# Attention with two chunks of scores at a time, their values and sums shifted, and output tiles in two parts

## What is computed

```
xn  = layernorm(x)
q   = xn @ q_w.T + q_b                       # 16 heads of 64
xd  = depthwise_conv(xn, width 3, stride 2)  # 2048 -> 1024 rows
k,v = xd @ k_w.T + k_b, xd @ v_w.T + v_b
att = softmax(q k^T / 8)                     # per head, 2048 x 1024
x1  = att v @ out_w.T + out_b
e   = argmax(xn @ W_router)                  # one of 4 experts per token
y   = gelu(xn @ W1[e] + b1[e]) @ Wo + bo + xn
out = x + x1 + layernorm(y) * ln_gamma + ln_beta
```

## Time and profile before

| | us |
|---|---|
| median of 3 runs | 1966.93 |
| lowest and highest | 1964.63, 2223.03 |
| the profiled execution | 1971.07 |
| its span, first to last instruction, slowest core | 1969.5 |
| spans of the eight cores | 1947.0 to 1969.5 |

### The profile page before, as it was taken

How to read it: one execution, slowest core, us unless ns; L and a number is a source line. 1 busy time by engine, 2 the same in 40 slices (tenths; PEclk the granted TensorE clock), 3 DMA queues, 4 the chain that set the end, 5 groups by cost and what they waited for, 6 DMA issues and landing times.

```text
span 1969.5 us, 37041 instructions; the slowest of 8 cores (1947.0 to 1969.5 us)
## 1 busy us (share of the span) xinstructions
PE 1828.8 (93%) x12540; PEld 1004.3 (51%) x12540; DVE 934.0 (47%) x1257; ACT 895.2 (45%) x1381; POOL 298.3 (15%) x357
## 2 busy tenths in 40 slices
PE   3588999998999999887899999999999999999995
PEld 1245222232554222222566666766666676666663
DVE  3354689856563888774132233413333323332225
ACT  2244988887455977775122222322222322222221
POOL 3122001001230110011001111101111111101111
PEclk9799999999999999998999999999999999999998
DMA  7759989984686999954756566856555776556551
GB/s 172 182 150 122 181 159 172 162 156 144 183 174 138 141 167 169 166 184 156 260 195 216 203 213 215 266 207 218 211 204 186 249 263 212 183 188 208 203 197 72
DMA packets 89171, 366.69 MB, mean 186 GB/s; under 512 B 11792, under 2 KB 11936, under 8 KB 68000
## 3 DMA queue, kind: packets, MB, share of 16 engines
q1 hardware_dynamic: 50112, 252.06, 38.8%
q0 software_dynamic: 38880, 112.27, 29.7%
HBM read 363.27 MB, written 94.90 MB: 233 GB/s over the span
## 4 chain that ended last, share of the span: by engine, by line
PE 73%; DMA 10%; DVE 6%; ACT 6%; issue 3%; POOL 0%; SPq 0%; DVEq 0%; ACTq 0%; POOLq 0%
PE ff_py L981 25%; PE ff_pu L946 25%; ACT pbuf L556 5%; DMA xa_d<-stg 4%; PE ps_a L505 4%; PE ps_s L543 4%; PE ps_a L569 4%; PE ps_q L367 3%; DMA row<-x 3%; DVE rc L581 3%; PE ps_q L395 2%; PE ps_m L574 2%; PE ps_q L381 2%; DMA xn_d<-row 2%; DMA stg<-x 1%
## 5 line engine op out<-in xcount | busy, mean ns | idle before, releaser
L960 ACT ACTIVATE ff_it<-ff_pu,b1t 128x256 bf16<-128x256 f32 (+1 forms) x608 | 244.3, 453 | 729.6 <-PE ff_pu L946 729.6
L556 ACT ACTIVATE pbuf<-ps_s 128x1024 bf16<-128x1024 f32 x512 | 477.3, 1061 | 116.8 <-PE ps_s L543 99.4
L946 PE MATMUL ff_pu<-ff_xg,ff_w 128*128 128x256 bf16 (+1 forms) x4864 | 516.4, 265 | 1.1 <-DVE ff_xg L930 1.1
L981 PE MATMUL ff_py<-ff_wo,ff_it 128*128 128x512 bf16 x2240 | 510.7, 381 | 3.8 <-DVE stg L511 3.8
L946 PEld LDWEIGHTS ff_pu<-ff_xg,ff_w 128*128 128x128 bf16 x4864 | 444.9, 98 | 73.4 <-issue 1.3
L981 PEld LDWEIGHTS ff_py<-ff_wo,ff_it 128*128 128x128 bf16 x2240 | 218.7, 98 | 238.2 <-issue 8.1
L581 DVE RECIPROCAL rc<-ps_m 128x512 f32<-128x512 f32 x64 | 214.7, 3355 | 44.9 <-PE ps_m L574 44.2
L569 PE MATMUL ps_a<-pbuf,v_sb 128*64 128x512 bf16 x1024 | 209.1, 404 | 5.8 <-DVE masks_all L464 4.8
L543 PE MATMUL ps_s<-qT,kT 64*128 64x512 bf16 x1024 | 201.3, 384 | 11.9 <-ACT pbuf L556 9.7
L574 PE MATMUL ps_m<-pbuf,ones 128*64 128x512 bf16 x1024 | 197.7, 381 | 0.0
L930 DVE COPY ff_xg<-ff_pt 128x1024 bf16<-128x1024 bf16 x35 | 24.2, 691 | 348.0 <-PE ff_pt L923 348.0
(11 more groups left out here) (135 smaller groups left out, 1238.7 us busy)
## 6 DMA issues: line engine op xcount, KB each, us to landing
ff_w<-scrW SPq DMA_DIRECT2D x152, 1024.0 KB
scrW<-w POOLq DMA_DIRECT2D x64, 512.0 KB, 15.6
row<-x SPq DMA_DIRECT2D x32, 512.0 KB, 6.6
xn_d<-row SPq DMA_DIRECT2D x32, 512.0 KB, 5.8
row<-xn_d SPq DMA_DIRECT2D x32, 512.0 KB, 15.8
stg<-x SPq DMA_DIRECT2D x32, 512.0 KB, 12.1
xa_d<-stg SPq DMA_DIRECT2D x32, 512.0 KB, 8.9
scrWo<-wo POOLq DMA_DIRECT2D x16, 512.0 KB, 13.0
```

The costliest lines, as they stand in the source:

```text
L556: e_at[g] = op("scalar", lambda s: s.activation(pbuf[g % 4][:, :], ps_s[g % 2][:, :], AF.Exp, scale=0.125), w)
L946: E.emit("tensor", lambda t, r_=r, q_=q, ic_=ic, c=cc, j_=j, sl=k % NW1SLOT: t.matmul(pu[r_][:, q_, 0:n], w1[:, sl, c * 512 + ic_ * 128:c ...
L960: E.emit("scalar", lambda s, r_=r, q_=q, ic_=ic, i_=i, j_=j, k_=k: s.activation(it[:, k_ % 3, ic_, 0:n], pu[r_][:, q_, 0:n], AF.Gelu, bias ...
L981: E.emit("tensor", lambda t, a_=a, o=oh, ic_=ic, i_=i, k_=k: t.matmul(py[:, 2 * a_ + o, :], it[:, k_ % 3, ic_, a_ * 128:(a_ + 1) * 128], w ...
```

## The change

The loop takes two chunks per round, g (even) and g + 1. It emits: exponential of g, scores of g + 1, scores of g + 2, exponential of g + 1, half of an output tile, the sums of g - 1, side work of both chunks, values of g, sums of g, values of g + 1. The sums of an odd chunk thus stand in the next round, and the reciprocal and multiplication of a pair (`divide`) follow them there. An output half tile is computed in two parts of four matmuls, at kc 4 and kc 6, in `ps_m` of the other parity instead of `ps_a`; what used that bank (transposes, prefix sum, position table) now uses `ps_a`. `flush_stores` runs at kc 0. The two steps of the routing that use TensorE are taken at kc 6 only, so the steps between shift a little.

```
-    ps_t = {i: bank(f"ps_t{i}", [128, CC, 128], BF16, i) for i in (5, 7)}
+    ps_t = {i: bank(f"ps_t{i}", [128, CC, 128], BF16, i) for i in range(4, 8)}
...
-    def out_unit(b, qb, u, si):
+    def out_part(b, qb, u, si, ocs):
...
-        for oc in range(CC):
+        at = 5 + 2 * si
+        for oc in ocs:
             m = op("tensor", lambda t, o=oc: t.matmul(
-                ps_a[si][:, :], otp[qb % 2][:, o, tt * 128:(tt + 1) * 128],
+                ps_m[si][:, :], otp[qb % 2][:, o, tt * 128:(tt + 1) * 128],
                 ow[:, o * D + oh * 512:o * D + (oh + 1) * 512], start=(o == 0), stop=(o == CC - 1)),
-                ([otp_at[(b, qb)], W["o"]] + K.bank[4 + 2 * si]) if oc == 0 else [], inc=oc == CC - 1)
+                ([otp_at[(b, qb)], W["o"]] + K.bank[at]) if oc == 0 else [], inc=oc == CC - 1)
+        if ocs[-1] < CC - 1:
+            return
...
         def values(g):
...
             if kc == 0:
-                w = w + K.bank[4 + 2 * si] + K.bank[5 + 2 * si]
+                w = w + K.bank[4 + 2 * si]
...
+        def sums(g):
+            P, kc = divmod(g, NKC)
+            si = P % 2
+            w = [e_at[g], m_ones] + (K.bank[5 + 2 * si] if kc == 0 else [])
             for h in range(2):
                 m = op("tensor", lambda t, h_=h: t.matmul(
                     ps_m[si][64 * h_:64 * (h_ + 1), :], ones64[:, :],
                     pbuf[g % 4][:, h_ * 512:(h_ + 1) * 512], start=(kc == 0), stop=(kc == NKC - 1)),
-                    inc=h == 1)
+                    w if h == 0 else [], inc=h == 1)
+            return m
+
+        def divide(P, m_sum, m_val):
...
+            m = op("vector", lambda v: v.reciprocal(rc[:, :], ps_m[si][:, :]), [m_sum] + K.rc)
+            K.bank[5 + 2 * si] = [m]
+            w = [m, m_val]
...
-        for g in range(NG):
+        def close(g):
+
+            m = sums(g)
+            pv_at[g] = pv_last[b] = m
+            if g % NKC == NKC - 1:
+                divide(g // NKC, m, val[g])
+
+        val = {}
+        for g in range(0, NG, 2):
...
             expo(g)
+            if g:
+                scores(g + 1)
             if g + 2 < NG:
                 scores(g + 2)
-            if kc == 5 and qb >= 1:
-                out_unit(b, qb - 1, hp, (P + 1) % 2)
-            if kc == 1:
+            expo(g + 1)
+            if kc in (4, 6) and qb >= 1:
+                out_part(b, qb - 1, hp, (P + 1) % 2, range(CC // 2) if kc == 4 else range(CC // 2, CC))
+            if g:
+                close(g - 1)
+            if kc == 0:
                 flush_stores()
             side(P, kc)
+            side(P, kc + 1)
             values(g)
+            pv_at[g] = sums(g)
+            val[g + 1] = values(g + 1)
+        close(NG - 1)
...
-            a_transpose(gt - 1, 5 + 2 * ((P + 1) % 2))
+            a_transpose(gt - 1, 4 + 2 * ((P + 1) % 2))
...
-        K.at = 5 + 2 * ((P + 1) % 2)
+        K.at = 4 + 2 * ((P + 1) % 2)
...
-            if kc in ((2, 6) if "texp" in M else (2, 4, 6)):
+            on_pe = "sum" not in M or M.get("left") == 2
+            if kc in ((6,) if on_pe else (2, 6) if "texp" in M else (2, 4, 6)):
                 step = next(rt)
+                M["sum"] = True
+                if step == "left":
+                    M["left"] = M.get("left", 0) + 1
```

More of the change, by code:

```diff
@@ L511, in out_unit @@
         m = op("vector", lambda v: v.tensor_tensor(
-            stg[s_][:, oh * 512:(oh + 1) * 512], ps_a[si][:, :], stg[s_][:, oh * 512:(oh + 1) * 512], op=ALU.add),
+            stg[s_][:, oh * 512:(oh + 1) * 512], ps_m[si][:, :], stg[s_][:, oh * 512:(oh + 1) * 512], op=ALU.add),
             [m, mx])
-        K.bank[4 + 2 * si] = [m]
+        K.bank[at] = [m]
         if oh == 1:
@@ L560, in values @@
             P, kc = divmod(g, NKC)
-            qb, hp = divmod(P, HP)
+            hp = P % HP
             si = P % 2
@@ L568, in values @@
             for h in range(2):
-                op("tensor", lambda t, h_=h: t.matmul(
+                m = op("tensor", lambda t, h_=h: t.matmul(
                     ps_a[si][64 * h_:64 * (h_ + 1), :], v_sb[:, kc, (2 * hp + h_) * 64:(2 * hp + h_ + 1) * 64],
                     pbuf[g % 4][:, h_ * 512:(h_ + 1) * 512], start=(kc == 0), stop=(kc == NKC - 1)),
-                    w if h == 0 else [], inc=False)
+                    w if h == 0 else [], inc=h == 1)
[4 more added lines that the diff above has]
+            w = [e_at[g], m_ones] + (K.bank[5 + 2 * si] if kc == 0 else [])
             for h in range(2):
@@ L619, in unit @@
         def unit(u):
-            out_unit(b, NQB - 1, u, u % 2)
+            out_part(b, NQB - 1, u, u % 2, range(CC))
             flush_stores()
```

32 lines of the change are left out of this document (15 added, 17 removed).

## The result

The changed kernel took 1990.82 us (median of four executions, 1989.39 to 2000.6). The ratio to the kernel before, from executions in turn on the same chip, is 1.0138 with a 95% interval of 1.0082 to 1.0194: slower by less than 2%, but surely slower. The lowest times differ by 24.8 us (1989.39 against 1964.63). Forecast were 1997 us and 29.7 us more. The profiled execution took 1990.12 us.

What follows compares the result with a forecast made beforehand. ScalarE was taken to bound pairs without output, TensorE and ScalarE in turn or VectorE those with output. Terms 12.6 + 13.4 + 3.5 + 0.2 = 29.7 us on 1966.93 gave 1997 us, range 1957 to 2013.

Steps and rivals of the forecast that it cites:

- The first pair of a block: First pair of a query block: output waits for the previous pair's last multiplication, +0.4 for five such pairs, 2.0 us.
- pair 0: First of the eight pairs without output in each batch, forecast +0.79 us like the others.
- pairs 28 to 31: Batch 0 pairs with normalisation on ScalarE and eight transposes: 10.63 to 11.5 us, four times 0.9, +3.5 us.
- the first pairs of batch 1: Pairs without output in batch 1: +0.79 us each, with the routing's preparation on VectorE left as it is.
- The wait of the odd values: Odd values start 1.71 us behind their scores; two chunks take 2.03, pairs without output 8.12 against 7.33, +12.6 us.
- Pairs with output: Pairs carrying an output half tile take 9.56 us against 9.01 or 9.16: 8.4 us in batch 0, 3.0 in batch 1.
- Batch 1, last pairs: Pairs 19 to 31: plain pairs +2.4, position table's wait 3.2 won, casts +1, sum +0.2 us; late load up to 5 won.
- 0.3 us of slack: Output's first part, its bank freed by the reciprocal at 4.65, waits for nothing until 5.00 in its pair.
- A: Rival: the wait at the odd value matmul does not bind; about -16 us, 1951 us; chance 0.12.
- B: Rival: weight loads show inside the runs of matmuls too, gaps 0.32 instead of 0.24; +23, 2020 us; chance 0.08.
- C: Rival: new order lowers TensorE's clock in steps with waits; 4 us, within the range; no chance of its own given.

Runs made afterwards that it cites:

- the first run: Against the changed kernel, values of the odd chunk moved one step later, beside its sums; profiled execution 1986.12 us, lowest 1983.14, no ratio.

## Why the prediction was right, and where its terms were off

The time came within 6 us and the side and the cause hold. That it came so near is in part luck: terms that were too small (the first pair of a block, pair 0) and terms that were too large (pairs 28 to 31, the first pairs of batch 1) cancel. The terms, each as the growth between the same two reciprocals, on the core of the earlier trace rows and as the difference of the medians over the eight cores:

| term | forecast | measured on that core | medians of eight cores |
|---|---|---|---|
| pairs 1 to 7, batch 0 | 5.5 (7 of 12.6 / 16) | 58.07 - 51.56 = 6.5 | 6.5 |
| pairs 8 to 27, batch 0 | 8.4 + 1.2 | 192.14 - 182.73 = 9.4 | 9.5 |
| pairs 28 to 31, batch 0 | 3.5 | 43.18 - 42.02 = 1.2 | 1.1 |
| pairs 1 to 7, batch 1 | 5.5 | 58.03 - 53.99 = 4.0 | 4.0 |
| pairs 8 to 18, batch 1 | 3.0 + 0.8 | 106.46 - 102.14 = 4.3 | 4.3 |
| pairs 19 to 31, batch 1 | 0.2 | 130.16 - 138.94 = -8.8 | 131.74 - 130.80 = 0.9 |

1. *The wait of the odd values.* Right, though the 0.79 a pair should have been 0.75 by the 7.37 that I had read for these pairs. 1.72 us from scores to values against 1.71, with all three parts of it as read in the trace of before: 0.55, 1.02, 0.14. The step is 2.05 and not 2.03, because a value matmul that starts out of a wait is followed by scores 0.34 later, not 0.32. That is 0.1 per pair. Two of the first seven intervals are 8.50, 0.3 more still. In the first the reciprocal of pair 0 came early in its step: its sums stand 0.68 behind the step's first scores (210.18 to 210.86), in later pairs 0.90. In the other an exponential starts 0.84 behind its scores instead of 0.55 (257.41 to 258.25), and no row names the cause. What I did not foresee is the second loop, through the score bank, which the first run laid bare at 7.88.

2. *Pairs with output.* 9.45 against 9.56. The gaps that no row had shown are 0.22 (scores to scores, at 276.04 and 276.27) and 0.22 to 0.24 (between sums and values, either way), just under the 0.24 that I took. That the products no longer bound the pair, since 9.17 fits into 9.45, held.

3. *The first pair of a block.* The mechanism was right, its term of 0.4 was mis-sized: it is 0.97 over a plain pair (10.42 - 9.45; the third of each batch 0.75). And there are six such pairs and not five: the sixth, pair 24 of batch 1, lies in the stretch of the last term. Three steps of the chain were each read too short. The reciprocal began 0.2 late, behind a product of the router. The multiplication followed 0.24 behind it and not 0.17. And the first output matmul came 0.36 behind the multiplication (349.71 to 350.07), where I had put 0.07 "with the semaphore". Together 0.6, which is the miss.

4. *Pairs 28 to 31.* The estimate of the new length, 11.5, was near (11.29, 11.34, 11.25), yet the term was three times too large. I took one pair, 10.63, as the length before for all four; the four reciprocals lie 10.87, 10.63, 10.66 and 9.87 apart. And the normalisation stands in only three of the four pairs; the last has transposes alone, and became shorter: 9.3. A term that is multiplied by four should have been read in four rows.

5. *Batch 1, first pairs.* I left the routing's preparation as it was and added the new wait on top. But pair 2 is 10.94 before and 11.00 after: VectorE sets it, and the steps' waits vanish in it and in the two pairs behind it (7.23, 7.22), where the others catch up. What VectorE holds up anyway cannot be held up twice; 1.5 us too much.

6. *Batch 1, last pairs.* The forecast had +0.2 with up to 5 us of gain kept for the lower end. On the core of the earlier trace rows it is -8.8, because there the pair of the position table went from 15.33 to 10.84 us and the add that waited for its load 5.45 us waits no longer. But that core was the exception: on the other seven no add of this stretch waited longer than 0.85 for its load in the kernel before, and the medians over the eight cores give +0.9. In the run with the later routing alone, which moves no store, one core still waited so, for 2.8 us. So this load costs the kernel only in an execution in which it hits the slowest core; whether the longer pairs or the moved stores bring the tile in time in the changed kernel, where no core waits, was not tried. The position table's wait is gone, as forecast, but the first part of the output tile in the same pair now waits 1.52 us for the reciprocal on six cores, the wait that I had given 0.3 us of slack (on the other two it waits 1.73, and the profile names the exponential). In this pair the granted clock was at 0.50 for 3.4 us on five of the eight cores, and the pair takes 12.43 us on these and 10.85 on the other three.

The six rows sum to 16.6 us on the core of the earlier trace rows, to 28.1 on core 7, the slowest of the changed kernel, and to 26.4 by the medians; the forecast for them was 28.1. From first to last exponential, median over the cores, the batches grew by 20.0 and 11.4; they include pair 0, which the reciprocals leave out and for which I had 0.8 per batch, where 2.9 and 2.1 are left. Between the batches 1.8 us were won. The spans of the two slowest cores differ by 19.0 us, but the medians of the eight spans by 28.7 (1956.3 and 1985.0), and the ratio gives 27: the core with the late load makes the profiled execution of before look slower than the kernel is.

*The rivals.* A (the wait does not bind) is refuted by the first reciprocals. The gain that it promised was tested by its own means: even with the odd values late, the second loop holds the pairs at 7.88. B (weight loads show inside the runs) is refuted: scores follow scores 0.22 apart while the second pair loads the rows in use, so there, too, a load overlaps with matmuls on its own row group. The Trainium skill, "TensorE: Matmul & The Clock Gate", Part 3, The mechanism, lets a load run ahead if its row group does not conflict or if it goes to the background weight buffer; I had weighed the first half alone. The trace contradicts that half alone and is compatible with the second; no row shows which buffer a load took. C (a lower clock) is refuted for the steps with waits: 1.00 in the attention stretches and 0.983 over the slowest core, against 0.981 before. Where the clock does fall is pair 28 of batch 1, before and after.

*Where the expected gain went.* The change takes up to 0.19 us per two chunks off TensorE's own work and gives it back, and more, as a wait for the exponential, because it shortens the distance between an odd chunk's scores and their use from two chunks of work to some one and a half (the forecast's 1.28 us of matmuls).

## What to carry to other kernels

Before work is regrouped to save gaps on an engine, write down for each operation how much other work lies between its input's producer and itself, and compare that with the producer's latency (here 0.55 + 1.02 + 0.14 us): a distance of two chunks was cover that no busy bar shows. An engine at 99% by modelled ends may have nothing to win; the idle time of the engine behind it, and the distance from start to start, tell who sets the pace. And take a change apart: here its smallest part, moving 32 small matmuls from chunk 2 to chunk 6, pays when made alone (0.9963, by the interval 0.04 to 0.7%), and in the whole change (1.0138) it cannot be seen. And read a term on all cores: one core's late load made -8.8 us of a +0.9.

## What the runs showed of the hardware that was not expected

- The gap between two matmul groups depends on whether the form of the half array changes: 0.22 us from scores to scores and 0.22 to 0.24 between sums and values, 0.31 to 0.32 when scores follow sums or values and when they are followed by them. The weight loads in question take 93 to 108 ns; about one such load seems to be exposed per change of form; that is inferred from the sizes and was not tried alone.
- A stalled group costs a little more than its wait: 0.34 instead of 0.31 from values to scores where the values had waited for ScalarE.
- Where the first matmul of a group waits for three semaphores instead of one (the values of pair 0), TensorE's wait instructions stand 0.106 us apart. With half the exponentials the steps of pair 0 are 1.84 us (204.14 to 205.98), later ones 1.64, so two further waits fit the difference; no run changed the number of waits alone.
- A matmul that had been waiting for VectorE started 0.36 us after the end of the multiplication, against 0.14 after the end of an exponential on ScalarE. The two were not compared in a run of their own.
- TensorE's granted clock fell to 0.50 for 3.4 us (6.8 on some cores) in pairs in which TensorE had stood still for longer than elsewhere: 3.74 us ahead of the position table before, on all eight cores. But the same wait did not always bring it: behind 1.52 us ahead of the output tile, pair 28 of batch 1 in the changed kernel ran with such a fall on some cores (12.43 us) and at 1.00 on others (10.85). A fall made a pair about 1.6 us longer there, and by as much in the kernel with the later routing alone (12.07 against 10.41) and in the one with late values (12.08 against 10.49).
